# Two attention layers in one kernel: a lead of fixed length for the row maxima, their high parts sent first, and full 512-column score products in the second attention stream

## The reference

```python
scores = jnp.einsum('bqhd,bkd->bhqk', q, k) * scale
alibi = slopes[:, None, None] * (pos_k - pos_q).astype(jnp.float32)
causal = pos_k <= pos_q
scores = jnp.where(causal[None, None], scores + alibi[None], NEG_INF)
probs = jax.nn.softmax(scores, axis=-1)
attn = jnp.einsum('bhqk,bkd->bqhd', probs, v).reshape(B, S, H)
```

## Time and profile before

| | us |
|---|---|
| median of 3 runs | 2327.37 (2321.92 to 2331.13) |
| profiled execution, its own time | 2315.58 |
| its span, first to last instruction | 2313.8 |
| TensorE busy in it | 2036.8 (88%) |
| VectorE busy | 1453.2 (63%) |
| ScalarE busy | 1160.9 (50%) |
| mean granted clock of TensorE | 0.906 |

### The profile page before, as it was taken

The page is one execution under the profiler, slowest core; times in us unless marked ns, Lnnn a source line. Parts: engine busy times, 40 slices in busy tenths (PEclk is TensorE's granted clock), DMA queues, the critical chain, the costliest instruction groups (busy, mean ns, idle before and its releaser), DMA issues. The chain is left out here.

```text
span 2313.8 us, 32000 instructions
## 1 busy us (share of the span) xinstructions
PE 2036.8 (88%) x12048; PEld 1192.4 (52%) x12048; DVE 1453.2 (63%) x2484; ACT 1160.9 (50%) x2431; POOL 134.2 (6%) x171
## 2 busy tenths in 40 slices
PE   7986999999999997879999986689999999998685
PEld 5772333333333333758888865544444444446564
DVE  5315999999999992844333335366666666644677
ACT  3211887887788885133222212146666666563153
POOL 0000000000000000300000000000000000001202
PEclk9995999999999999979999997868878888877898
DMA  5444332332422401250101004423122122102411
GB/s 212 155 150 61 43 51 38 52 47 33 61 38 36 58 6 55 97 173 29 37 1 37 19 9 168 125 33 46 26 47 45 28 47 38 34 2 73 146 51 73
DMA packets 97706, 143.58 MB, mean 62 GB/s; under 512 B 28900, under 2 KB 40036, under 8 KB 97408
## 3 DMA queue, kind: packets, MB, share of 16 engines
q1 hardware_dynamic: 96440, 139.35, 25.7%
q10 hardware_dynamic: 728, 1.41, 0.4%
q0 software_dynamic: 384, 0.77, 0.1%
HBM read 93.91 MB, written 47.05 MB: 61 GB/s over the span
## 5 line engine op out<-in xcount | busy, mean ns | idle before, releaser
L753 DVE TENSOR_REDUCE maxesB<-s_psB 128x1 f32<-128x1024 f32 x512 | 603.0, 1220 | 95.3 <-PE s_psB L780 85.0
L718 ACT ACTIVATE probsB<-st_psB 128x512 f32<-128x512 f32 x1024 | 528.6, 603 | 131.3 <-PE st_psB L791 130.9
L750 DVE CUSTOM_DVE_ANT_0 junkG<-s_psG,ramp 128x896 bf16<-128x896 f32 (+7 forms) x512 | 366.1, 755 | 214.9 <-PE s_psG L780 213.5
L780 PE MATMUL s_psB<-k_stackB,q_stackB 48*128 48x512 f32 x1024 | 409.5, 480 | 28.3 <-DMA k_stackB<-k_parts 19.3
L718 ACT ACTIVATE probsG<-st_psG 128x512 f32<-128x512 f32 (+3 forms) x768 | 334.7, 495 | 189.4 <-PE st_psG L802 102.6
L791 PE MATMUL st_psB<-q_stackB,k_stackB 50*128 50x512 f32 x1024 | 376.6, 452 | 33.0 <-ACT probsB L718 5.8
L780 PE MATMUL s_psG<-k_stackG,q_stackG 52*128 52x512 f32 (+3 forms) x768 | 271.2, 463 | 61.3 <-DVE maxesG L750 21.2
L791 PE MATMUL st_psG<-q_stackG,k_stackG 54*128 54x512 f32 (+3 forms) x768 | 299.0, 471 | 10.7 <-ACT probsG L718 6.5
L780 PEld LDWEIGHTS s_psB<-k_stackB,q_stackB 48*128 48x128 f32 x1024 | 173.5, 190 | 244.6 <-DVE maxesB L753 168.1
L824 PE MATMUL o_psB<-probsB,v_onesB 128*32 128x512 f32 x2048 | 274.3, 608 | 0.0
L791 PEld LDWEIGHTS st_psB<-q_stackB,k_stackB 50*128 50x128 f32 x1024 | 168.7, 185 | 138.8 <-ACT probsB L718 119.4
(11 more groups left out here) (240 smaller groups left out, 2824.3 us busy)
## 6 DMA issues: line engine op xcount, KB each, us to landing
q_stackB<-q_parts SPq DMA_DIRECT2D x93, 128.0 KB
k_stackB<-k_parts SPq DMA_DIRECT2D x93, 128.0 KB
q_stackG<-q_parts SPq DMA_DIRECT2D x93, 128.0 KB
q_parts<-partsA SPq DMA_DIRECT2D x16, 512.0 KB, 2.8
k_parts<-partsA SPq DMA_DIRECT2D x16, 512.0 KB, 2.8
q_parts<-partsF SPq DMA_DIRECT2D x16, 512.0 KB, 2.8
k_stackG<-k_parts SPq DMA_DIRECT2D x93, 64.0 KB
xA<-in_x SPq DMA_DIRECT2D x4, 1024.0 KB
```

The costliest lines, as they stand in the source:

```text
L718: act.activation(probs[:, (i % ring) * GH + h, first:HALF], st_ps[:, n % n_st, first:HALF], ACT.Exp).then_inc(st_used, 1)
L750: dve.tensor_tensor_reduce(junk[:, n % JUNK, 0:width], scores, ramp[:, SEQ - width:SEQ], 1.0, LOWEST, ALU.add, ALU.max, out).then_inc(maxe ...
L753: dve.reduce_max(out, scores, AX.X).then_inc(maxed, 1)
L780: ins = pe.matmul(s_ps[:, slot_of[n] + part, 0:b - a], qst[at, it % 3, half, h % GS, qt * P:(qt + 1) * P], kst[at, it % 3, h % kh, a:b], s ...
```

## The change

Three edits. `LEAD` is no longer a number of steps but a length, 3400, in the units of the steps' cost. SyncE sends the two high rows as soon as ScalarE has made them, and the low ones when GpSimd has. Row scores always stream 512 keys and key scores all 512 columns of the bank, also where the mask or `first` leaves fewer in use; who reads them reads the same columns as before. `step_order` counts 512 for each. Layer 0's products had 512 columns before.

```diff
-LEAD = 3
+LEAD = 3400
...
-        ahead = max(done[UNITS * (t + 1) - 1] - (rate * ends[first_of[t] - LEAD - 1] if t else 0) for t in range(3))
+        ahead = max(done[UNITS * (t + 1) - 1] - rate * max(ends[first_of[t] - 1] - LEAD if t else 0, 0) for t in range(3))
...
             if item[0] == "row":
-                x, y = row_parts(*units[item[1]][:2])[item[2]]
-                free[u] += y - x
+                free[u] += HALF
             else:
-                free[u] += HALF - first if item[0] == "key" else SIDE * (item[2] + 1)
+                free[u] += HALF if item[0] == "key" else SIDE * (item[2] + 1)
...
                 it, half = divmod(t, 2)
-                sp.wait_ge(m_parts, t + 1)
                 if t:
                     sp.wait_ge(m_rows, n_rows * t)
-                for p in range(SHIFT):
+                for p, made in enumerate((m_high, m_parts)):
+                    sp.wait_ge(made, t + 1)
                     for u in range(SIDES):
...
-                a, b = row_parts(t, qt)[part]
+                a = HALF * part
...
-                ins = pe.matmul(s_ps[:, slot_of[n] + part, 0:b - a], qst[at, it % 3, half, h % GS, qt * P:(qt + 1) * P],
-                                kst[at, it % 3, h % kh, a:b], start=True, stop=True)
+                ins = pe.matmul(s_ps[:, slot_of[n] + part, :], qst[at, it % 3, half, h % GS, qt * P:(qt + 1) * P],
+                                kst[at, it % 3, h % kh, a:a + HALF], start=True, stop=True)
...
-                ins = pe.matmul(st_ps[:, n % n_st, first:HALF], kst[at, it % 3, h % kh, kt * P:(kt + 1) * P],
-                                qst[at, it % 3, half, h % GS, first:HALF], start=True, stop=not diagonal)
+                ins = pe.matmul(st_ps[:, n % n_st, :], kst[at, it % 3, h % kh, kt * P:(kt + 1) * P],
+                                qst[at, it % 3, half, h % GS, :], start=True, stop=not diagonal)
```

More of the change, by code:

```diff
@@ L569, in step_order @@
     def step_order(i):
-        _, _, _, first, diagonal = steps[i]
+        diagonal = steps[i][4]
         keys = [[h for h in range(GH) if h // GS == u] for u in range(SIDES)]
@@ L785, in key_scores @@
             def key_scores(i, h):
-                it, half, kt, first, diagonal = steps[i]
+                it, half, kt, _, diagonal = steps[i]
                 n = where["exp", i, h]
```

## The result

| | before | after |
|---|---|---|
| median of 7 runs, us | 2321.92 | 2300.62 (2294.30 to 2308.44) |
| span of the profiled execution | 2313.8 | 2298.7 |
| second stream's stage, first to last instruction | 615.4 | 597.3 |
| first stream's stage | 729.1 | 727.9 |
| mean granted clock | 0.906 | 0.929 |

The ratio is 0.990, with a 95% interval of 0.9876 to 0.9923: 1% less, which is clear of the scatter but small. It is 21 us on the medians and 15 on the two profiled executions, where 67 were forecast.

What follows compares the result with a forecast made beforehand. TensorE bounds the kernel, with the chain through ScalarE inside a step, its clock falling behind a DMA wait. Iterations -60, last iteration -10, starts +3: -67 us on 2315.58, put at 2260 us; range 2230 to 2305.

Steps and rivals of the forecast that it cites:

- second rival: Second stream: clock falls in some iterations because five and six row products wait on VectorE; 2300 us, chance 0.12.
- The wait's chain: Second stream, ahead of each second half: turn issued a step earlier, so TensorE's 0.93 us wait for the maxima's DMA goes.
- The iteration at full clock, 31.7: Second stream: 29.7 at full clock, 1.7 for added columns, 0.3 for row units; 4.0 us less than 35.69.
- If the clock stays up: Second stream's iterations: without the DMA wait the clock holds; full-clock length 29.7 us against 35.69, before added columns.
- The last iteration, -10: Second stream's last iteration, without row scores: full clock saves 9 us and the wait 1, so 10 (5 to 12).
- The starts, +3: Stream starts: more maxima ahead 3.5 us, wide products at half clock 1, less 1.4 + 1; together +2 to +3.
- Layer 0: First stream: 31 waits by weight loads are covered, steps stay at 2.60 to 2.61 us; a gain of 1 us taken.
- first rival: Second stream: clock falls all the same, from thin short diagonal steps or stack-load DMA traffic; 2351 us, chance 0.12.
- rule against this: Trainium skill: only idle gaps well longer than 0.93 us let the clock fall, so removing this wait should not help.

Runs made afterwards that it cites:

- e3: Only the full columns, with the old lead of three steps and old row order, against the kernel before: ratio 0.985, median 2293.30 us.
- e1: Only the longer lead on the kernel before, products narrow, high rows not sent early: ratio 0.973, median 2281.07 us.
- e6: The changed kernel with narrow key scores again, wide row scores kept: ratio 0.976 to the kernel before, median 2264.73 us.
- e7: The changed kernel with narrow row scores again, wide key scores kept: ratio 0.989 to the kernel before, median 2294.47 us.
- e5: e4 with row units spread more evenly over the second stream's steps: ratio 0.981 to the kernel before, median 2278.79 us.
- e9: e5 with narrow key scores: ratio 0.965 to the kernel before, median 2246.11 us.
- e4: The changed kernel plus unread row products in the second stream's last iteration: ratio 0.983 to the kernel before, median 2286.19 us.
- e11: The changed kernel itself measured once more: ratio 0.989 to the kernel before, median 2300.63 us.
- e2: Longer lead and high rows first on the kernel before, products narrow: ratio 0.985, median 2291.62 us.

## Why the prediction was wrong

The direction was right, and the DMA wait went as forecast. But the clock did not stay up, and so the size was wrong: 2260 was forecast, 62 us under the median of the seven executions before, and 21 were gained. 2300.62 lies in the range, 4 us from its upper end, and is the second rival's time, though partly by luck: the rival put 33 us on falls in seven or eight iterations and 9 on the last one, where falls in five cost 15.6, the last one 14.6, and a longer clean iteration the other 16. By the prediction's steps, on the profiled executions:

- **The wait's chain.** Right. The wait went, the high rows saved 0.75 us where 0.7 was forecast. What was missed: the full columns remove the wait as well (e3), since they lengthen the two steps it hides under. I summed the two edits as if only one touched the wait.
- **The iteration at full clock, 31.7.** It is 32.7 to 32.8: inside 29.7 to 33.1. Two terms were small: without added columns it is 30.6 (e1), not 29.7 + 0.3, and the columns cost 2.1 (e6, e7), not 1.7. The first was the guess for the two steps over the second half's start: put at 2.28 and 2.2, they take 2.66 and 2.61 in e1, with waits of 0.53 and 0.55 for VectorE in them. Over 15 iterations 16 us.
- **"If the clock stays up".** This is the step that failed. The prediction took the fall for a result of one wait. It fell in 5 of 15 iterations in the crowded steps, behind two shorter waits for VectorE: the place and the circumstances that the second rival named, for seven or eight iterations. It cost 15.6 us (506.95 less 15 clean iterations of 32.76; 0.9 of it in the first iteration, which begins at half clock). That the crowding is the cause is shown by e5 and e9, where the row products are spread out and 28 of 28 iterations hold. That the waits in it are, is not: the clean iterations have the same two, and e1's, longer ones.
- **The last iteration, -10.** It came to +4.6 (38.7 against 34.1). This is the second place of the same failure. I took the steps without row products of the first stream, at 2.60 and full clock, as proof that the second's would hold too. They don't: the clock fell at the first value product, before any DMA wait. And the proof was the luck of one trace, since the first stream's own steps of this kind lost the clock in seven of thirteen profiled executions, for up to 11 us. 14.6 us; e4 shows that the missing row products are the cause and gives 12 back.
- **The starts, +3.** The second stream's start, from its first row product to its first value product, takes 36.3 us for 31.9: it cost 4.4, where the terms for it came to 2.6. The full columns at half clock cost 1.8 (e3's 22.7 less 20.8), not 1. ScalarE's table load behind the second turn, which I had not followed, has no price of its own in these runs.
- **Layer 0.** Not shown either way. Its stage is 1.2 us shorter, but in six profiled executions with the same layer 0 (the change, e4 to e7, e11) it takes 727 to 736 us. Its steps at full clock stay at 2.60 to 2.61.

The sum: 16 + 15.6 + 14.6 + 1.8 is 48 of the 52 us between -67 and -15; the rest lies in stretches that the change does not touch. The lower end of the forecast's sum is -102, not -101 (90 + 12).

The first rival's mechanism, that thin products themselves let the clock fall, may have a share: it fits the falls of e1 and e2 in the first steps, which the full row scores prevent, and e4's last iteration, where more streaming held the clock through the same waits. Its other mechanism, the stack loads, is excluded by e5. Its price, slower than before, came nowhere. My rule against this, that the idle gap is too short, was not borne out: the clock fell behind a gap of 0.93 in all 16 iterations before, and behind pairs of 0.35 and 0.52 in some iterations after. The same page of the Trainium skill, "TensorE: Matmul & The Clock Gate", has a section that fits better, on a second failure mode, psum-queue depth-cycling: short idle times between groups of products, repeated, make the clock oscillate. The trace after looks like that, with the waits of 0.35 and 0.52 us for free score banks as the idle times, but e1 held the clock in the same steps through 0.53 and 0.55. I had weighed the section that reassured me about short waits and not this one.

What stays open: why the same schedule, with the same two waits, falls in one iteration and not in the next; which part of the crowding, the waits or what is streamed between them, decides; and why the clock's first rise in the stream came 22.6 us after the first value product in e5 (at 1564.0), and 1.7 us after it in e4.

## What to carry to other kernels

Where the clock falls, look at the whole stretch and every short wait in it, not at the longest wait alone: with that one gone the clock can still fall, and two edits that both stretch or shorten the time around one wait don't add. Spread work that waits on another engine evenly over the steps, and give an engine that runs out of work at a stream's end something harmless to do; both cost next to nothing and together brought 22 us on top of the change's 21, on the medians. Widen the products that stream beside the chain (rows: 0.7 us), not those in it (keys: 1.4 us). And don't take steps at full clock in one trace as proof that they always keep it: compare several executions.

## What the runs showed of the hardware that was not expected

Work that nobody reads made the last iteration 12 us shorter (38.7 to 26.6), by the clock alone. In steps with waits of only 0.35 and 0.52 us the clock was lost in 19 of 42 iterations (the change, e4, e11), for up to 13.7 us, while in e1 it never fell in these steps, with two waits of 0.53 and more: the length of the waits alone does not tell. Steps of 2.60 us that are the same each time kept the clock in six profiled executions and lost it in seven (layer 0's last ones). And a kernel whose steps are the same to 0.01 us from iteration to iteration can still scatter by 3% between executions (e1), and its mean granted clock, 0.885 to 0.930, moves with them.
